# Layer norms joined with the recurrence, the local passes and the fire attention that they feed

## What is computed

```
x = x + 0.5 * moe(layernorm(x))               # 8 experts, 2 of them weighted, per token
x = x + rglru(layernorm(x))                   # the recurrence, below
x = x + 0.5 * moe(layernorm(x))
x = x + 0.5 * local_transformer(layernorm(x)) # 6 layers: windowed attention, gated feed-forward
x = x + fire_attention(layernorm(x))          # causal attention with a learned distance bias
x = x + 0.5 * local_transformer(layernorm(x))

# recurrence: w_in and w_a have 8 diagonal blocks of 16x16
gate_x, gate_a = sigmoid(x @ w_in + b_in), sigmoid(x @ w_a + b_a)
log_a = -8 * gate_a * softplus(a_param)
a, mult = exp(log_a), sqrt(1 - exp(2 * log_a))    # at the first token of a sequence: a = 0, mult = 1
h[t] = a[t] * h[t-1] + x[t] * gate_x[t] * mult[t]
```

## Time and profile before

| | us |
|---|---|
| median of 3 runs | 4131.73 (4127.85 to 4132.27) |
| the profiled execution | 4129.52 |
| its span (first to last instruction) | 4127.7 |

### The profile page before, as it was taken

How to read it: one execution, slowest core, us unless ns; L and a number is a source line. 1 busy time by engine, 2 the same in 40 slices (tenths; PEclk the granted TensorE clock), 3 DMA queues, 4 the chain that set the end, 5 groups by cost and what they waited for, 6 DMA issues and landing times. The chain is left out here.

```text
span 4127.7 us, 167239 instructions
## 1 busy us (share of the span) xinstructions
PE 3725.9 (90%) x66080; PEld 2917.0 (71%) x66080; DVE 3163.1 (77%) x6467; ACT 3270.4 (79%) x10763; POOL 2608.6 (63%) x2482
## 2 busy tenths in 40 slices
PE   8958969999999999999995886999999999999996
PEld 7947947777777777777773655777777777777773
DVE  2243248888888888888874877888888888888884
ACT  4434439998999999999982676999999999999994
POOL 0000028777777787777761647777877878777772
PEclk9988979999999999999996898999999999999998
DMA  1000013334333333333330003334333333333341
GB/s 39 19 1 24 19 43 112 118 103 120 99 111 118 105 120 96 112 117 106 120 91 8 1 1 115 117 104 120 107 103 119 102 113 113 103 120 97 111 119 37
DMA packets 547030, 361.36 MB, mean 88 GB/s; under 512 B 32320, under 2 KB 532816, under 8 KB 546000
## 3 DMA queue, kind: packets, MB, share of 16 engines
q1 hardware_dynamic: 546256, 350.66, 28.4%
HBM read 248.59 MB, written 101.97 MB: 85 GB/s over the span
## 5 line engine op out<-in xcount | busy, mean ns | idle before, releaser
L1285 POOL TENSOR_TENSOR lt_t<-lt_t,lt_rn 128x512 f32<-128x512 f32 x768 | 786.5, 1045 | 666.2 <-DVE lt_rn L1140 664.6
L1016 ACT ACTIVATE lt_pb<-lt_pb,lt_mx 128x64 f32<-128x64 f32 x3072 | 1022.4, 342 | 0.0
L1279 POOL TENSOR_TENSOR lt_t<-lt_t 128x512 f32<-128x512 f32 x768 | 972.1, 1287 | 12.1 <-DVE lt_t L1114 12.0
L49 PE MATMUL ps<-lt_wh,lt_xh 128*128 128x512 f32 (+1 forms) x1536 | 578.5, 377 | 83.2 <-POOL lt_xl L1258 57.9
L1016 ACT ACTIVATION_READ_ACCUMULATOR lt_pb<-lt_pb,lt_mx 128x1 f32 x3072 | 598.9, 195 | 0.0
L996 ACT ACTIVATE lt_qkT<-ps 128x512 f32<-128x512 f32 x768 | 459.4, 598 | 132.8 <-PE ps L816 132.6
L1125 DVE TENSOR_REDUCE lt_ss<-lt_sq 128x8 f32<-128x512 f32 x768 | 520.3, 678 | 41.2 <-ACT lt_sq L991 35.6
L1114 DVE TENSOR_TENSOR lt_t<-ps,lt_tab 128x512 f32<-128x512 f32 x768 | 526.0, 685 | 4.3 <-issue 1.4
L1120 DVE TENSOR_TENSOR lt_t<-ps,lt_tab 128x512 f32<-128x512 f32 x768 | 522.6, 680 | 4.0 <-PE ps L816 2.5
L51 PE MATMUL ps<-lt_wh,lt_xl 128*128 128x512 f32 (+1 forms) x1536 | 521.1, 339 | 0.0
L816 PE MATMUL ps<-ident,lt_t 128*128 128x128 f32 x3072 | 478.8, 278 | 46.1 <-ACT lt_qkT L996 41.6
(11 more groups left out here) (213 smaller groups left out, 7462.9 us busy)
## 6 DMA issues: line engine op xcount, KB each, us to landing
lt_vw<-v_scratch SPq DMA_DIRECT2D x768, 256.0 KB, 3.7
v_scratch<-lt_vv SPq DMA_DIRECT2D x384, 256.0 KB, 2.1
lt_wraw<-in_lt_wqkv SPq DMA_DIRECT2D x56, 384.0 KB, 6.0
moe_w<-in_moe_w SPq DMA_DIRECT2D x32, 256.0 KB, 2.9
lt_wo<-in_lt_wo SPq DMA_DIRECT2D x48, 128.0 KB, 3.9
lt_w<-in_lt_w SPq DMA_DIRECT2D x12, 341.0 KB, 4.3
lt_w<-in_lt_w SPq DMA_DIRECT2D x12, 192.0 KB, 3.6
lt_gl<-in_lt_qs SPq DMA_DIRECT2D x2, 768.0 KB, 7.1
```

Of the source, the lines that this page charges most:

```text
L49: nc.tensor.matmul(out, lh, rh, start=start, stop=False)
L1016: ins = nc.scalar.activation(p, p, ACT.Exp, bias=mx[:, par, c:c + 1], accum_out=sm[:, par, c:c + 1])
L1279: nc.gpsimd.tensor_tensor(o, o, t2[:, t, :], ALU.add).then_inc(padd[t], 1)
L1285: nc.gpsimd.tensor_tensor(o, o, rn[:, u[1] % 2, 8 * t:8 * t + 8].unsqueeze(2).to_broadcast([P, 8, DH]), ALU.mult).then_inc(qkd[t], 1)
```

## The change

Four of the seven norms are no longer blocks of their own. `recurrence_phase`, `local_transformer_phase` and `fire_attention_phase` now call `layer_norm_block` with their own context, semaphores and buffers (`owner`, `room`), and hand it their set-up work as functions: `loads` (SP), `setup` (GpSimd), `after_scale` and `after_squares` (ScalarE), `tables` and `finish` (VectorE). The set-up blocks are gone, and so is the clear after those four norms; the seven semaphores are cleared with the phase's own.

In all seven norms the order by chunk is new: TensorE alternates means and variances, ScalarE does Ln and Exp of a chunk together, and loads one table set (`natural_log_exp_and_others`) by hand at the start. With `add_shifted`, the additions are spread between the chunks. The recurrence loads wa first; gives the a gate to TensorE and ScalarE first; moves gx*XN and the addition to M to GpSimd; and does the product, the scan and the addition by chunks of 512 columns. In the local transformer the subtractions of groups 2 and 3 and of w1 move from the set-up block into GpSimd's list of the main block, behind `split_batch(0, 0)`; the wait for the tables moves there too.

```diff
-def layer_norm_block(nc, res, src, dst, add_shifted=None):
+def layer_norm_block(nc, res, src, dst, add_shifted=None, room=None, owner=None, loads=None, setup=None,
+                     after_squares=None, after_scale=None, tables=None, finish=None):
...
+                mean(0)
+                mean(1)
                 for c in range(NC):
-                    pe.wait_ge(sq_done, c + 1)
-                    nc.tensor.matmul(bank[4 + c][:, :], avg[:, :], sq[:, c * CH:(c + 1) * CH],
-                                     start=True, stop=True).then_inc(var_done, 1)
+                    variance(c)
+                    if c + 2 < NC:
+                        mean(c + 2)
...
+                if add_shifted is not None:
+                    add(0)
+                    add(1)
+                for c in range(NC):
+                    deviation(c)
+                    if add_shifted is not None and c + 2 < NC:
+                        add(c + 2)
+                    if c == 2:
+                        scaled(0)
+                if tables is not None:
+                    tables(dve)
+                for c in range(1, NC):
+                    scaled(c)
+                if finish is not None:
+                    finish(dve)
...
+                def scale(c):
+                    act.wait_ge(var_done, c + 1)
+                    nc.scalar.activation(rstd[:, cols(c)], bank[4 + c][:, :], ACT.Ln, bias=eps[:, 0:1]).then_inc(log_done, 1)
+                    act.wait_ge(log_done, c + 1)
+                    nc.scalar.activation(rstd[:, cols(c)], rstd[:, cols(c)], ACT.Exp, scale=-0.5).then_inc(rstd_done, 1)
+                nc.scalar.preload_act_table_set("natural_log_exp_and_others")
+                square(0)
+                square(1)
                 for c in range(NC):
...
+                    scale(c)
+                    if after_scale is not None:
+                        after_scale(act, c)
+                    if c + 2 < NC:
+                        square(c + 2)
+                    if c == 1 and after_squares is not None:
+                        after_squares(act)
...
@@ recurrence_phase
+        layer_norm_block(nc, res, M, plain(XN), owner=(ctx, sems), loads=first_loads, setup=first_zeros,
+                         after_squares=first_softplus, tables=finish_softplus, room=(ga, th, den))
...
             @block.scalar
             def _(act):
                 for c in range(NC):
+                    act.wait_ge(ga_p, c + 1)
+                    nc.scalar.activation(ga[:, cols(c)], bank[4 + c][:, :], ACT.Sigmoid, bias=vec[:, 1:2]).then_inc(ga_d, 1)
+                    act.wait_ge(ga_d, c + 1)
+                    nc.scalar.activation(th[:, cols(c)], ga[:, cols(c)], ACT.Tanh, scale=v[:, 6:7]).then_inc(th_d, 1)
                 for c in range(NC):
+                    act.wait_ge(gx_p, c + 1)
+                    nc.scalar.activation(gx[:, cols(c)], bank[c][:, :], ACT.Sigmoid, bias=vec[:, 0:1]).then_inc(gx_d, 1)
                 for c in range(NC):
+                    nc.scalar.activation(a[:, cols(c)], ga[:, cols(c)], ACT.Exp, scale=v[:, 7:8]).then_inc(a_d, 1)
                 for c in range(NC):
                     act.wait_ge(ratio_d, c + 1)
+                    nc.scalar.activation(th[:, cols(c)], th[:, cols(c)], ACT.Sqrt, scale=2.0).then_inc(mult_d, 1)
...
-                nc.vector.tensor_tensor(gx[:, :], gx[:, :], th[:, :], ALU.mult).then_inc(nx_d, 1)
-                dve.wait_ge(nx_d, NC + 1)
-                nc.vector.tensor_tensor_scan(h[:, :], a[:, :], gx[:, :], 0.0, ALU.mult, ALU.add).then_inc(scan_d, 1)
-                dve.wait_ge(scan_d, 1)
-                nc.vector.tensor_tensor(M[:, :], M[:, :], h[:, :], ALU.add)
+                def scan(c):
+                    s = cols(c)
+                    dve.wait_ge(a_d, c + 1)
+                    dve.wait_ge(mult_d, c + 1)
+                    nc.vector.memset(a[:, c * CH:(c + 1) * CH:T], 0.0).then_inc(fix_d, 1)
+                    nc.vector.memset(th[:, c * CH:(c + 1) * CH:T], 1.0).then_inc(fix_d, 1)
+                    dve.wait_ge(fix_d, 2 * c + 2)
+                    dve.wait_ge(nx_d, c + 1)
+                    nc.vector.tensor_tensor(gx[:, s], gx[:, s], th[:, s], ALU.mult).then_inc(in_d, 1)
+                    dve.wait_ge(in_d, c + 1)
+                    nc.vector.tensor_tensor_scan(h[:, s], a[:, s], gx[:, s], 0.0, ALU.mult, ALU.add).then_inc(scan_d, 1)
+                ratio(0)
+                ratio(1)
+                for c in range(NC):
+                    scan(c)
+                    if c + 2 < NC:
+                        ratio(c + 2)
+
+            @block.gpsimd
+            def _(pool):
+                for c in range(NC):
+                    pool.wait_ge(gx_d, c + 1)
+                    nc.gpsimd.tensor_tensor(gx[:, cols(c)], gx[:, cols(c)], XN[:, cols(c)], ALU.mult).then_inc(nx_d, 1)
+                for c in range(NC):
+                    pool.wait_ge(scan_d, c + 1)
+                    nc.gpsimd.tensor_tensor(M[:, cols(c)], M[:, cols(c)], h[:, cols(c)], ALU.add)
...
@@ local_transformer_phase
+        def first_loads(sp):
+            load_group(sp, 0, 0)
+            load_group(sp, 0, 1)
+            qs = bass.AP(tensor=d["lt_qs"].tensor, offset=0, ap=[[0, P], [1, DEPTH * 4 * DH]])
+            sp.dma_start(gl[:, :, :].rearrange("p k n -> p (k n)"), qs).then_inc(qsld, 16)
+            load_group(sp, 0, 2)
+            load_group(sp, 0, 3)
+            load_columns(sp, w1, "lt_w1", 0, 0, w1ld)
...
+        def first_high(act, c):
+            high_group(act, 0, c)
+            if c == GJ - 1:
                 high_up(act, 0)
...
+        def first_low(pool):
+            nc.gpsimd.memset(vv[0:WIN, :, :, :], 0.0).then_inc(ipad, 1)
+            nc.gpsimd.memset(qkT[:, :, :, 0:WIN], 0.0)
+            low_group(pool, 0, 0)
+            low_group(pool, 0, 1)
...
+        layer_norm_block(nc, res, M, shifted(X), owner=(ctx, sems), loads=first_loads, setup=first_low,
+                         after_scale=first_high, tables=make_tables,
...
+                dve.wait_ge(tabd, DEPTH)
                 dve.wait_ge(fvlld, 16)
...
                 split_batch(0, 0)
+                low_group(pool, 0, 2)
+                low_group(pool, 0, 3)
+                low_up(pool, 0)
...
@@ fire_attention_phase
+        layer_norm_block(nc, res, M, plain(XN), add_shifted=X, owner=(ctx, sems), loads=first_loads, setup=first_fill,
+                         after_squares=first_logs, tables=first_floor, finish=first_lengths,
```

318 lines of the change are left out of this document (138 added, 180 removed).

## The result

The changed kernel takes 4064.15 us (median of 4 runs, 4063.07 to 4069.55); the kernel before, beside it on the same chip, 4130.69 (4 runs, 4127.85 to 4132.27). The ratio is 0.9842, 95% interval 0.9825 to 0.9859: 66.5 us faster. Forecast were 4070, in 4052 to 4092. The profiled execution took 4065.2 us around a span of 4063.4.

What follows compares the result with a forecast made beforehand. TensorE bounds the passes (busy 90% of the span); the norm stretches between, 218.4 us, are chains of waiting engines. Gains of 62.0 less 1.5 for semaphores give 60.5 off 4129.5, 4069.0; forecast 4070, range 4052 to 4092.

Steps and rivals of the forecast that it cites:

- Norms 1, 3 and 7: Norms that stay alone: table loads go and chunks interleave; 3.0, 2.8 and 0.5 us gained.
- The low clock: Rival, in the norms: interleaved products keep TensorE slow, 3.4 us a norm, 17 us in all, 4087; chance 0.12.
- The drain: Rival: each table-set switch also drains about 1.38 us, so 11 us more is gained, 4059; chance 0.05.
- Norm 2 and the recurrence: Joined, DMAs hidden beside the norm: 65.1 us falls to 51.4, 13.7 gained, bounds 10 to 15.
- The gap: In the recurrence, VectorE idles 3.6 us between ratio 1 and scan 0, until ScalarE's first Sqrt.
- VectorE's stalls beside GpSimd: In the recurrence, 0.6 us added for VectorE held up beside GpSimd, making 35.5 us.
- Norms 4 and 6: Joined with the local set-ups, VectorE the path: 20.2 and 20.6 us, 17.2 and 15.3 gained, bounds 13 and 18.
- GpSimd into the pass: At the pass's start, three moved subtractions, 5.8 us, fit GpSimd's idle 5.69: 0.2 us late or nothing.
- without that gap: At the pass's start, lacking GpSimd's idle 5.69 us, the moved subtractions would make it 5.8 us late.
- Norm 5: Joined with the fire set-up, DMAs beside the norm: 20.1 us of 29.6, 9.5 gained, bounds 7.5 and 11.
- The passes: The two passes keep their code but for GpSimd's first microseconds: 1605 to 1612 us, spread 7 either way.
- The shared ports: Rival: each GpSimd instruction stops VectorE for its length, in recurrence, joins and pass starts; 20 us, 4090; chance 0.16.

Runs made afterwards that it cites:

- A: The kernel before plus one line: norms load the Ln and Exp table set by hand, order and blocks unchanged; 4120.56 us, ratio 0.9975.
- F: The changed kernel with ratio 2 ahead of scan 0 and ratio 3 behind it in the recurrence; 4066.32 us, ratio 0.9846.
- B: The changed kernel without the line that loads the table set by hand; 4105.11 us, ratio 0.9932.
- C: The changed kernel with the local set-up back in its own block behind norms 4 and 6; 4077.67 us, ratio 0.9868.
- J: The changed kernel with three more unread GpSimd subtractions behind those moved to the pass's start; 4077.91 us, ratio 0.9869.
- N: The changed kernel with all of GpSimd's set-up subtractions beside norms 4 and 6, none left for the pass; 4078.53 us, ratio 0.9877.
- G: The changed kernel with only the first layer's rotary table made beside the norm, the others at the pass's start; 4072.76 us, ratio 0.9865.
- D: The changed kernel with the recurrence's GpSimd products and additions back on VectorE; 4072.69 us, ratio 0.9864.

## Why the prediction was right, step by step

**Norms 1, 3 and 7.** Norm 3 came as worked out (2.7 for 2.8), and A shows that the mechanism was the forecast one: 2.4 of the two loads' 2.57 come back. Norm 1 gave 1.0 more than worked out, and that is chance. TensorE was busy for 9.29 us instead of the 9.95 that the prediction took over from the kernel before, and the last variance waited 0.6 instead of 1.2. But A, in the old order, had its means in 5.38 us instead of 6.51, and equal code takes 12.9 to 14.1 in this norm: the forecast 14.1 (13.1 and a clear) is one end of that, the measured 13.1 near the other. One reading of the prediction is not borne out as it stands: it calls the first products of the earlier trace rows products at the low clock, while the granted clock of every microsecond in which they run is 1.00, in both kernels. What shows them slow is their length, 1.06 us a half at first and later 0.59. Norm 7 was worked out at 15.3 without its clear, came at 15.1, and was then shaded to 0.5 of gain out of doubt about the clock; the row was right and the shading wrong.

**The low clock** as a rival had the interleaved order keep TensorE slow, at 3.4 us a norm. TensorE was busy for 9.29, 9.70, 10.21, 10.21, 10.84 and 10.31 us in norms 1, 3, 4, 5, 6 and 7, where the kernel before has 9.93, 9.03, 8.78, 10.24, 9.75 and 10.04: 0.6 less to 1.4 more. So it falls in size. It is not nothing: slow products ahead of the first gate cost up to 1.8 us (F).

**The drain** falls, by A and B: 1.2 to 1.3 us a load, whether two go or eight come.

**Norm 2 and the recurrence**: 51.9 against 51.4. The gap stood where it was put, 3.35 for 3.6. The 0.6 for VectorE's stalls beside GpSimd was too small: one scan paid 0.94 and one product 0.56 (1.25 for 0.69). That the sum came within 0.5 us is partly luck, since equal code takes 49.5 to 51.9. No run takes this join apart; the rows alone show where its gain lies: 10.0 us passed between the norm's last scaling and ScalarE's first instruction of the recurrence, and 0.3 do now. No run takes norm 5's join apart either.

**Norms 4 and 6**: 20.0 and 20.5 against 20.2 and 20.6. VectorE has its first scaling and last deviation behind it at 9.97 us (8.7 or 10.4 were forecast: the subtraction does hold it up), tables 4.7 (between the 3.7 and 7.44 that bounded them), scalings 5.2, the border 0.3. ScalarE is done 15.5 us in (15 to 16 forecast). What the prediction didn't say is how little of these 17 us is the overlap: 6.2 (C). The rest is the norm's own chunks and loads (5.5), its clear (1.0), and a set-up that is shorter by itself (4.7), by the early `lt_gl` and by fewer subtractions beside the tables. In equal code these joins take up to 21.0 and 22.0, so the match to 0.2 is partly luck as well.

**GpSimd into the pass**: the wait fell from 5.69 to 0.71, not to nothing. The first addition does start 0.2 us later in the pass, as forecast, but because VectorE's result came later, not because GpSimd was busy. J shows that the next 4.9 us would have cost 3. The prediction's "without that gap" was right as a limit, and the change sits just under it.

**Norm 5**: 19.4 against 20.1. ScalarE reached the logs at 11.8 (12.0), the last Exp ended at 16.4 (17.0), and everything behind was early by the same 0.6. `first_logs` stands ahead of chunks 2 and 3, as forecast, and costs VectorE a wait of 2.2 us.

**The passes** are where the forecast's 0 was neither shown nor refuted: -5.8 and +4.2, -1.6 together with a clear. This sum is chance of the two profiled executions: with the same code the first pass took 1605.9 and 1606.0 and the second 1608.8 and 1611.8. The mixture of experts' +1.0 is of that kind: 226.3 to 227.9 with equal code.

**The shared ports** as a rival gave 4090. Its mechanism is there, and nearly in the size it gave to one stop: a subtraction of 1.82 costs the four scalings 1.5, and two of them cost 3.2 (J, norm 6). It was wrong in the number of stops. Measured: 1.5 us per join in the scalings and some 1 in the tables (4.69 for six; undisturbed, in J's second join, 3.69), 1.5 in the recurrence, where two of the additions run beside a reciprocal that keeps its 3.35, and no sign of it at the passes' start, where the rival had 11.6 of its 20 us. That is 6 to 7 us, most of it already in the sum. N and G show the rival's mechanism where it does decide: tables 7.91 and 7.28.

The forecast missed the median by 5.9 us: 3.8 are the sum's (64.3 for 60.5), 1.0 lies between its 4069.0 and the 4070 taken, and 1.05 between this kernel's profiled execution and its median. The 3.8 are norms 1, 5 and 7 (2.2), the passes with a clear (2.1 beyond the forecast) and the fire attention (0.8), less the recurrence (0.5) and the experts (0.9); norms 3, 4 and 6 are off by 0.1 together. No step failed. The terms that were mis-sized beyond what equal code spreads by are the stalls beside GpSimd (0.6 for 1.5) and norm 5 (20.1 for 19.4); the miss in norm 1 is within that spread. A total that is off by 5.9 us can't confirm single terms of 1 us; what confirms them is the waits that went where they were forecast to go.

What stays open: why D's median is 6 to 9 us over the changed kernel's with 0.6 in its stretch, why TensorE's first products are slow for a longer or shorter time, and why the end of a pass takes 52 to 59 us from the last store; the granted clock differs there between executions too, and nothing was tried on it.

## What to carry to other kernels

Stretches between two dense loops are worth reading as timelines even when they are 5% of the span: here all of a 1.6% gain came from idle time there. The parts that runs show are the local set-ups run beside their norms (12 us for both, C) and a table set that is no longer chosen anew for each function (10 us, A); a load issued two places too late was 2.5 us in each set-up. Before an operation is put beside another to hide it, ask which engine is the path there and whether the two share SBUF: a VectorE product of two SBUF tiles beside a GpSimd subtraction costs both. And when an edit's worth (3 us) is under the kernel's own spread (7 us), measure its stretch in the trace, not the total, and start the stretch behind whatever varies with equal code: F's 3.6 us were 1.8 once both kernels were counted from the same instruction.

## What the runs showed of the hardware that was not expected

- VectorE and GpSimd hold each other up, each for about as long as the other's instruction still runs. Four scalings take 1.72 us alone, 3.24 beside one subtraction of 1.82, and 4.91 beside two. The last scan of the recurrence shows both sides: GpSimd's addition, begun beside a product of 0.69, takes 1.81 instead of 1.26, and runs 1.08 us into the scan, which takes 2.17 instead of 1.22. A scalar addition takes 0.40 alone and 1.49 beside a product of GpSimd; six products 3.69 alone, 4.69 with two subtractions near and 7.91 with more. GpSimd's subtraction takes 1.8 alone and 2.2 to 2.3 in the crowd. A reciprocal beside an addition keeps its 3.35.
- At a pass's start TensorE's clock was granted at 0.50 to 0.94 for the first 20 us and more, another way in most executions, and the sixteenth store came some 0.45 us later per us of clock lost, a spread of 4.7 us in equal code. Products whose results nobody reads raised the clock to 0.83 and then 0.88 to 1.00, and gained nothing.
- The first products of a norm are slow for a time that differs between executions of equal code: the eight halves of means took 5.37 to 6.51 us in the first four norms of the two kernels that have them in a row (before and A).
- Without the line that loads a set by hand, Ln and Exp in turn each had a load ahead, 31 in the first four norms (B), though one set holds both: with the line they ran without any.
